# Moving the norm statistic into the projection loop, shifting the dequantising jobs, and a third FC1 weight buffer

## The chip, the cores and the metric

The kernel runs on the 8 cores of one Trainium2 chip, one batch element on each, with no traffic between them. The time is that of the device in microseconds, of the slowest core. Before the change the median of 3 runs is 1756.84 us (1755.2 to 1759.04).

## The reference, cut to what matters

```
x:  8 x 2048 x 1024
xn = layernorm(x)
q, k, v = xn @ Wq, xn @ Wk, xn @ Wv          # 16 heads of 64
q, k = rope(q), rope(k)
s  = softmax(causal(q @ k.T / 8)) @ v @ Wo
h  = layernorm(xn) * gamma + beta
w1 = (fc1_q - 128) * fc1_scales              # 1024 x 4096, int32 and scales per 128 rows
w2 = (fc2_q - 128) * fc2_scales              # 4096 x 1024
g  = silu(xn + 0.5 * (silu(h @ w1 + b1) @ w2 + b2))
out = x + s * g
```

## The kernel before, in words

Everything is issued in an order written out by hand: `sch.op` appends an instruction to one engine's stream, `sch.wait` appends a wait on a semaphore to it, and each engine works its stream in order. A block (`run_block`) ends with all engines meeting.

**Block b2** first projects v, then runs the projection loop (L485 to L558): 8 rounds `it`, 4 for q and 4 for k, each for 4 heads. A round has 4 strips `tgq` of 512 tokens. A strip is 16 matmuls on TensorE (L502, L507), two evacuations on ScalarE (L518, L520), and the rotation on VectorE, six operations (L526 to L541) into `qe_s` and `qo_s`. Strip 2 reuses the PSUM half of strip 0, so its matmuls wait for strip 0's evacuation. After strip 3 ScalarE issues eight DMAs (L550, L553) that put the round's heads in place in `q_att` or `k_att`; VectorE waits for the eight of the round before (L524) before it overwrites `qe_s`. Between rounds SyncE loads the next weights and VectorE casts them (L480).

Then comes the norm loop (L567 to L596), which finds the largest squared norm over pairs of heads for a safe softmax offset. For each of 8 head pairs of q and of k: a Square on ScalarE (L572), four matmuls with ones into `p6` (L579), a `reduce_max` (L585) and a running maximum on VectorE (L593). The Square of one waits for the matmuls of the one before.

**Block b3, attention.** 32 groups (4 query stretches `qg` of 512, 8 head pairs `m`), with K = 4, 8, 12, 16 key tiles a group as `qg` rises. For each key tile TensorE makes the scores (L733), ScalarE the exponentials (L752), GpSimd masks the last 4 tiles of a group (L762, L764), TensorE sums values and denominators (L782, L790). The epilogue of a group is split: its reciprocals (L803) and casts (L808) are queued on VectorE in the next group, and the broadcast matmul (L815), the copy to `rep_sb` (L823) and the product (L827) at that group's end. Between two groups stands a batch of the 48 dequantising jobs: SyncE loads the integers and the scales into one buffer each, VectorE forms the product (L688), GpSimd issues the store (L693). Jobs 0 to 15 are for w1 (2048 columns), 16 to 47 for w2 (1024 columns). A job's VectorE operation waits for the store of the job before, since there is one output buffer. How many jobs are due after group `gidx` is one line:

```
L847  want = min(ndq, (ndq * gidx + 31) // 32)
```

**Block b3, output projection and FC1.** 16 token tiles `tt` of 16 matmuls with Wo (L934, L938); from `tt` 2 on four FC1 visits stand behind each (L914, 8 matmuls of 512 columns), 64 visits in all. A visit needs 256 KB of w1 in one of two buffers `w1t3`, loaded on SyncE's queue once the visit two before is through:

```
L899  if vi >= 2:
L900      sch.wait("sync", "cPE", pe_y[vi - 2])
```

The same stretch loads `h_fm`, `w2a` and `w2b`.

**Block b4** has FC2 for the first 1024 tokens (L1068, L1072), FC1 for the second 1024 (L1038, 32 weight loads into two buffers `w1t`), FC2 for them, and the elementwise end.

Of the kernel before, what the change touches and what calls it, by code (L numbers as in the profile page):

```python
# [7 lines left out]
F32 = mybir.dt.float32  # L8
# [6 lines left out]
S = 2048  # L15
# [3 lines left out]
F = 4096  # L19
# [74 lines left out]
def build_nc(upto=9):  # L94
# [31 lines left out]
    with ExitStack() as es:  # L126
# [239 lines left out]
        with ExitStack() as ps:  # L366
# [83 lines left out]
            rp_t = [sb(ps, f"rp_t{i}", 1024, BF16) for i in range(2)]  # L450
            sch.wait("vector", "cGP", gp_hm[NCH - 1])
# [31 lines left out]

            emit_slab_loads(0)
            for ti, (w_d_, att) in enumerate(((wq_d, q_att), (wk_d, k_att))):  # L485
                for cp in range(4):
                    it = ti * 4 + cp
                    wp = it % 2
                    if it + 1 < 8:
                        emit_slab_loads(it + 1)  # L490
# [3 lines left out]
                    for tgq in range(4):  # L494
# [49 lines left out]
                        gp_rope[(it, tgq)] = sch.snap("cVE")  # L544
                    ve_rope_all = sch.snap("cVE")
# [14 lines left out]
            nsq = [qe_s, qo_s]  # L560
            sch.wait("scalar", "dR0")
            sch.wait("scalar", "dR1")
            sch.wait("scalar", "cVE")
            first_nmax = {0: True, 1: True}
            sc_nsq = {}
            pe_nmm = {}
            for ti, att in enumerate((q_att, k_att)):  # L567
                for m in range(8):
                    im = 8 * ti + m
                    if im >= 1:  # L570
                        sch.wait("scalar", "cPE", pe_nmm[im - 1])
                    sch.op("scalar", lambda e, att=att, m=m, im=im: e.activation(  # L572
                        nsq[im % 2][:], att[:, S * m:S * (m + 1)], AF.Square), inc="cSC")
                    sc_nsq[im] = sch.snap("cSC")
                    sch.wait("tensor", "cSC", sc_nsq[im])
                    if im >= 1:
                        sch.wait("tensor", "cVE")
                    for tgq in range(4):
                        sch.op("tensor", lambda e, tgq=tgq, im=im: e.matmul(  # L579
                            p6[0:1, :], ones_bf[:],  # L580
                            nsq[im % 2][:, 512 * tgq:512 * (tgq + 1)],
                            start=(tgq == 0), stop=(tgq == 3)), inc="cPE")
                    pe_nmm[im] = sch.snap("cPE")
                    sch.wait("vector", "cPE", pe_nmm[im])
                    sch.op("vector", lambda e: e.reduce_max(  # L585
                        stat[:1, 12:13], p6[0:1, :], axis=AX.X), inc="cVE")
                    sch.wait("vector", "cVE")
                    if first_nmax[ti]:
                        sch.op("vector", lambda e, ti=ti: e.tensor_copy(
                            stat[:1, 10 + ti:11 + ti], stat[:1, 12:13]), inc="cVE")  # L590
                        first_nmax[ti] = False
                    else:
                        sch.op("vector", lambda e, ti=ti: e.tensor_max(  # L593
                            stat[:1, 10 + ti:11 + ti],
                            stat[:1, 10 + ti:11 + ti], stat[:1, 12:13]), inc="cVE")
                    sch.wait("vector", "cVE")  # L596
# [27 lines left out]
        with ExitStack() as ps:  # L624
# [7 lines left out]
            lrec = sb(ps, "lrec", 512, F32)  # L632
            lrecb = sb(ps, "lrecb", 512, BF16)
            rep_sb = sb(ps, "rep_sb", 512, F32)
# [14 lines left out]
            with ExitStack() as ds:  # L649
# [58 lines left out]
                for qg in range(NQG):  # L708
                    for m in range(8):
# [137 lines left out]
                        want = min(ndq, (ndq * gidx + 31) // 32)  # L847
# [11 lines left out]
                for eng in ("sync", "vector", "scalar", "gpsimd"):  # L859
                    sch.wait(eng, "cVE", ve_dq_all)  # L860
                    sch.wait(eng, "dG0")
                    sch.wait(eng, "dG1")
            with ExitStack() as ws:
                w1t3 = [sb(ws, f"w1t3_{i}", NCH * 128, BF16) for i in range(2)]
# [31 lines left out]
                def emit_fc1_visit(vi):  # L896
                    ph, oc = fc1_visits[vi]
                    wb = w1t3[vi % 2]
                    if vi >= 2:  # L899
                        sch.wait("sync", "cPE", pe_y[vi - 2])  # L900
                    sch.op("sync", lambda e, oc=oc, wb=wb: e.dma_start(
                        out=wb[:],
                        in_=bass.AP(w1dram, 1024 * oc,
                                    [[NCH * F, 128], [128, 8], [1, 128]])), inc=f"dW{vi % 2}", k=16)
                    dwv = sch.snap(f"dW{vi % 2}")
# [3 lines left out]
                    sch.wait("tensor", f"dW{vi % 2}", dwv)  # L909
# [76 lines left out]
        with ExitStack() as ps:  # L986
# [9 lines left out]
            w1t = [sb(ps, f"w1t{i}", NCH * 128, BF16) for i in range(2)]  # L996
# [7 lines left out]
            for oc in range(2):  # L1004
                sch.op("sync", lambda e, oc=oc: e.dma_start(
                    out=w1t[oc][:],
                    in_=bass.AP(w1dram, 1024 * oc,
                                [[NCH * F, 128], [128, 8], [1, 128]])), inc=f"dW{oc % 2}", k=16)
                dw_pre[oc] = sch.snap(f"dW{oc % 2}")
# [7 lines left out]
            for p in range(NP):  # L1017
                if p == 1:
                    pe_v2 = {}
                    sc_y2 = {}  # L1020
                    for oc in range(NFC):
                        wb = w1t[oc % 2]
                        if oc >= 2:
                            sch.wait("sync", "cPE", pe_v2[(oc - 2, 1)])
# [3 lines left out]
                                            [[NCH * F, 128], [128, 8], [1, 128]])), inc=f"dW{oc % 2}", k=16)  # L1028
                            dw_now = sch.snap(f"dW{oc % 2}")
                        else:  # L1030
                            dw_now = dw_pre[oc]
                        sch.wait("tensor", f"dW{oc % 2}", dw_now)
# [170 lines left out]
```

How the kernel before makes its waits and increments, by code:

```python
            def g(e, fn=fn, h=c.h, k=k):  # L49
                fn(e).then_inc(h, k)
# [4 lines left out]
    def wait(self, eng, name, val=None):  # L55
        c = self.ct[name]
        v = c.n if val is None else val
        self.streams[eng].append(lambda e, h=c.h, v=v: e.wait_ge(h, v))
```

## Time and profile before

| | |
|---|---|
| median of 3 runs | 1756.84 us (1755.2 to 1759.04) |
| the profiled execution | 1761.0 us |
| its span, slowest core (all: 1730.4 to 1759.4) | 1759.4 us |
| TensorE busy with matmuls | 1173.9 us, 67% |
| VectorE busy | 627.5 us, 36% |
| ScalarE busy | 553.9 us, 31% |
| GpSimd busy | 303.9 us, 17% |
| mean granted TensorE clock, by core | 0.834 to 0.840 |

The shares are means over stages with different limits; what a change is worth is read inside the stage that it touches. Positions such as 349.61 are microseconds from the span's start on the slowest core. A number in brackets with an arrow is how long the engine had been idle and whose work it waited for. The granted clock is a mean over a stretch of two levels, 1.2 and 2.4 GHz.

### The profile page before, as it was taken

How to read it: one execution, taken by the hardware profiler on the slowest of the kernel's cores; microseconds unless marked ns; L12 is line 12 of the kernel's file. 1: busy time of each engine (PE TensorE's matmuls, PEld its weight loads, DVE VectorE, ACT ScalarE, POOL GpSimd, SP SyncE). 2: the span in 40 equal slices, each digit the busy share in tenths (PEclk: the TensorE clock that was granted, in tenths of full speed). 3: DMA queues.
4: the chain of work that ended last, by engine and by line, in shares of the span. 5: the costliest groups of instructions: out<-in, count | busy, mean ns of one | idle time of the engine just before them, and what ended most of it. 6: DMA issues, size and time to landing. Idle time of an engine off the chain costs nothing. (4 is left out here: it accounts for less than half of the span.)

```text
span 1759.4 us, 16319 instructions; the slowest of 8 cores (1730.4 to 1759.4 us)
## 1 busy us (share of the span) xinstructions
PE 1173.9 (67%) x5250; PEld 427.6 (24%) x5250; DVE 627.5 (36%) x674; ACT 553.9 (31%) x609; POOL 303.9 (17%) x574
## 2 busy tenths in 40 slices
PE   0004798774423345667877888667887998599994
PEld 0003243331000011111212222223333443244442
DVE  2132645543126666566545444500000112000123
ACT  1133012113422234546767777312122100243000
POOL 0100700000033333232232222300000132100230
PEclk9999999885555556767788888789999999799998
DMA  5655214441075566333322222374533322223223
GB/s 155 124 166 162 89 48 109 103 96 28 0 199 195 183 210 204 118 128 103 108 90 91 90 90 91 118 247 122 165 114 108 126 83 97 86 76 90 69 76 119
DMA packets 83922, 205.72 MB, mean 117 GB/s; under 512 B 16496, under 2 KB 33152, under 8 KB 78464
## 3 DMA queue, kind: packets, MB, share of 16 engines
q1 hardware_dynamic: 66096, 147.51, 27.0%
q10 hardware_dynamic: 8864, 29.38, 5.4%
q0 software_dynamic: 8880, 27.79, 5.1%
q8 instruction: 45, 0.74, 0.2%
q14 instruction: 37, 0.30, 0.1%
HBM read 163.21 MB, written 37.76 MB: 114 GB/s over the span
## 5 line engine op out<-in xcount | busy, mean ns | idle before, releaser
L752 ACT ACTIVATE ptb<-pbig,negub 128x1024 bf16<-128x1024 f32 x320 | 336.3, 1119 | 291.0 <-PE pbig L733 290.8
L782 PE MATMUL p<-ptb,v_tm 128*64 128x512 bf16 x640 | 158.2, 486 | 177.6 <-POOL ptb L764 90.0
L803 DVE RECIPROCAL lrec<-p 1x512 f32<-1x512 f32 x64 | 214.0, 3344 | 1.0
L733 PE MATMUL pbig<-q_att,k_att 64*128 64x512 bf16 x640 | 149.8, 482 | 36.3 <-ACT ptb L752 35.3
L914 PE MATMUL p<-h_fm,w1t 128*128 128x512 bf16 x512 | 129.3, 409 | 52.4 <-DMA w1t<-w1deq 44.3
L790 PE MATMUL p<-ptb,ones_bf 128*1 128x512 bf16 x640 | 146.9, 455 | 0.0
L1093 DVE TENSOR_SCALAR t_f<-xb,negmu_a,r_a 128x1024 f32<-128x1024 f32 x16 | 13.0, 812 | 348.0 <-PE p L1072 205.8
L764 POOL TENSOR_TENSOR ptb<-ptb,msk_bf 128x128 bf16<-128x128 bf16 x256 | 111.0, 439 | 104.8 <-ACT ptb L752 104.6
L1038 PE MATMUL p<-h_fm,w1t 128*128 128x512 bf16 x512 | 113.0, 384 | 22.8 <-ACT y_sl L1046 22.4
L688 DVE SCALAR_TENSOR_TENSOR dq_o<-dq_i,dq_s 128x1024 bf16<-128x1024 int32 (+1 forms) x48 | 75.6, 1575 | 146.7 <-DMA w2deq<-dq_o 68.0
L1119 POOL TENSOR_TENSOR f_sb<-f_sb,sb 128x1024 f32<-128x1024 f32 x13 | 30.5, 2345 | 508.5 <-ACT f_sb L1111 508.5
L332 PE MATMUL pT<-idn_bf,xnb 128*128 128x128 bf16 x128 | 16.2, 306 | 151.8 <-DVE xnb L324 148.7
L782 PEld LDWEIGHTS p<-ptb,v_tm 128*64 128x64 bf16 x640 | 40.7, 114 | 278.8 <-issue 278.8
L923 ACT ACTIVATE y_sl<-p,b_cm 128x512 bf16<-128x512 f32 x64 | 44.0, 687 | 168.6 <-PE p L914 168.5
L502 PE MATMUL pbig<-xn_fm,wE 128*128 128x512 bf16 x256 | 70.6, 425 | 31.9 <-ACT qeo L520 29.1
L1111 ACT ACTIVATE f_sb<-f_sb 128x1024 f32<-128x1024 f32 x16 | 16.9, 1057 | 228.9 <-DVE f_sb L1104 228.9
L914 PEld LDWEIGHTS p<-h_fm,w1t 128*128 128x128 bf16 x512 | 51.4, 104 | 128.3 <-issue 81.1
L1038 PEld LDWEIGHTS p<-h_fm,w1t 128*128 128x128 bf16 x512 | 50.4, 99 | 85.2 <-issue 27.3
L823 DVE COPY rep_sb<-p 128x512 f32<-128x512 f32 x32 | 22.1, 691 | 127.9 <-PE p L815 127.9
L1046 ACT ACTIVATE y_sl<-p,b_cm 128x512 bf16<-128x512 f32 x64 | 43.9, 687 | 73.2 <-PE p L1038 67.5
L507 PE MATMUL pbig<-xn_fm,wO 128*128 128x512 bf16 x256 | 66.5, 407 | 0.0
L733 PEld LDWEIGHTS pbig<-q_att,k_att 64*128 64x128 bf16 x640 | 31.5, 97 | 139.6 <-issue 139.6
(140 smaller groups left out, 1514.1 us busy)
## 6 DMA issues: line engine op xcount, KB each, us to landing
xb<-x SPq DMA_DIRECT2D x48, 512.0 KB, 4.5
w1t<-w1deq SPq DMA_DIRECT2D x96, 256.0 KB, 2.8
dq_i<-fc_q SPq DMA_DIRECT2D x16, 1024.0 KB, 5.5
dq_s<-fc_scales SPq DMA_DIRECT2D x16, 1024.0 KB, 9.0
dq_i<-fc_q SPq DMA_DIRECT2D x32, 512.0 KB, 4.0
dq_s<-fc_scales SPq DMA_DIRECT2D x32, 512.0 KB, 5.0
w1deq<-dq_o POOLq DMA_DIRECT2D x16, 512.0 KB, 9.7
w2deq<-dq_o POOLq DMA_DIRECT2D x32, 256.0 KB, 5.5
```

The source lines that it names most:

```text
L502: sch.op("tensor", lambda e, fc=fc, tgq=tgq, pe_=pe_, wp=wp: e.matmul(pe_, wE[wp][:, 128 * fc:128 * (fc + 1)], xn_fm[:, S * fc + 512 * tgq ...
L507: sch.op("tensor", lambda e, fc=fc, tgq=tgq, po_=po_, wp=wp: e.matmul(po_, wO[wp][:, 128 * fc:128 * (fc + 1)], xn_fm[:, S * fc + 512 * tgq ...
L688: sch.op("vector", lambda e, cols=cols, bi=bi: e.scalar_tensor_tensor(dq_o[bi][:, 0:cols], dq_i[bi][:, 0:cols], -128.0, dq_s[bi][:, 0:cols ...
L733: dst=(sc0 if jj == 0 else sc1): e.matmul(dst, k_att[r:r + 64, S * m + 128 * kt:S * m + 128 * (kt + 1)], q_att[r:r + 64, S * m + 512 * qg: ...
L752: sch.op("scalar", lambda e, pt=pt, half=half: e.activation(pt[:, 0:1024], pbig[:, 1024 * half:1024 * half + 1024], AF.Exp, bias=negub[:, ...
L764: sch.op("gpsimd", lambda e, pt=pt, base=base, off=off: e.tensor_mul(pt[:, base + off:base + off + 128], pt[:, base + off:base + off + 128 ...
L782: K=K, gp=gp: e.matmul(obank[gp][cpos:cpos + 64, :], v_tm[:, 1024 * kt + 64 * h:1024 * kt + 64 * (h + 1)], pt[:, 512 * (cpos // 64):512 * ...
L790: sch.op("tensor", lambda e, pt=pt, jj=jj, kt=kt, K=K, gp=gp: e.matmul(bass.AP(lbank[gp], 32 * jj * 512, [[512, 1], [1, 512]]), ones_bf[:] ...
L803: sch.op("vector", lambda e, jj=jj, gp=gp: e.reciprocal(lrec[32 * jj:32 * jj + 1, :], bass.AP(lbank[gp], 32 * jj * 512, [[512, 1], [1, 512 ...
L914: sch.op("tensor", lambda e, fc=fc, ph=ph, wb=wb, yp=yp: e.matmul(yp[:], wb[:, 128 * fc:128 * (fc + 1)], h_fm[:, S * fc + 512 * ph:S * fc ...
L923: sch.op("scalar", lambda e, oc=oc, ph=ph, yp=yp: e.activation(y_sl[:, 1024 * oc + 512 * ph:1024 * oc + 512 * (ph + 1)], yp[:], AF.Silu, b ...
L1038: sch.op("tensor", lambda e, fc=fc, ph=ph, wb=wb, yp=yp: e.matmul(yp[:], wb[:, 128 * fc:128 * (fc + 1)], h_fm[:, S * fc + 1024 + 512 * ph: ...
```

## The change

Four edits. **A.** The sixteen norms leave the loop of their own: in round `it` of the projection loop, from 1 on, the two norms of round `it - 1` are made, the first Square at the head of the round in ScalarE's stream, the rest after strip 1 is queued; the last two stay behind the loop. There is one scratch buffer `nsq_b`. **B.** The number of jobs due after a group follows another rule. **C.** The FC1 weights of block b3 rotate over three buffers, in space given back by `lrec`, `lrecb` and `rep_sb`. **D.** The same in block b4.

```diff
+            nsq_b = sb(ps, "nsq_b", S, BF16)
...
+            def emit_norm_sq(itx):
+                ti_x, cp_x = itx // 4, itx % 4
+                att_x = q_att if ti_x == 0 else k_att
+                for j2 in range(2):
+                    im = 8 * ti_x + 2 * cp_x + j2
+                    m = 2 * cp_x + j2
+                    if im >= 1:
+                        sch.wait("scalar", "cPE", pe_nmm[im - 1])
+                    sch.wait("scalar", f"dR{itx % 2}", dr_rep[(itx, 3)])
+                    sch.op("scalar", lambda e, att_x=att_x, m=m: e.activation(
+                        nsq_b[:], att_x[:, S * m:S * (m + 1)], AF.Square), inc="cSC")
+                    sc_nsq[im] = sch.snap("cSC")
+                    break
+
+            def emit_norm_mm(itx, j2):
...
+                if j2 == 1:
+                    if im >= 1:
+                        sch.wait("scalar", "cPE", pe_nmm[im - 1])
+                    sch.op("scalar", lambda e, att_x=att_x, m=m: e.activation(
+                        nsq_b[:], att_x[:, S * m:S * (m + 1)], AF.Square), inc="cSC")
+                    sc_nsq[im] = sch.snap("cSC")
+                sch.wait("tensor", "cSC", sc_nsq[im])
+                if im >= 1:
+                    sch.wait("tensor", "cVE", ve_nrm[im - 1])
+                for tgq in range(4):
+                    sch.op("tensor", lambda e, tgq=tgq: e.matmul(
+                        p6[0:1, :], ones_bf[:],
+                        nsq_b[:, 512 * tgq:512 * (tgq + 1)],
+                        start=(tgq == 0), stop=(tgq == 3)), inc="cPE")
+                pe_nmm[im] = sch.snap("cPE")
+                sch.wait("vector", "cPE", pe_nmm[im])
+                sch.op("vector", lambda e: e.reduce_max(
+                    stat[:1, 12:13], p6[0:1, :], axis=AX.X), inc="cVE")
+                sch.wait("vector", "cVE")
...
+                ve_nrm[im] = sch.snap("cVE")
...
                     wp = it % 2
+                    if it >= 1:
+                        emit_norm_sq(it - 1)
...
                         gp_rope[(it, tgq)] = sch.snap("cVE")
+                        if tgq == 1 and it >= 1:
+                            emit_norm_mm(it - 1, 0)
+                            emit_norm_mm(it - 1, 1)
...
-            for ti, att in enumerate((q_att, k_att)):
-                for m in range(8):
...
+            emit_norm_sq(7)
+            emit_norm_mm(7, 0)
+            emit_norm_mm(7, 1)
...
-                        want = min(ndq, (ndq * gidx + 31) // 32)
+                        if gidx <= 12:
+                            want = min(ndq, gidx // 3)
+                        else:
+                            want = min(ndq, 4 + (gidx - 12) * (ndq - 4) // 20)
...
+            ax.close()
             with ExitStack() as ws:
-                w1t3 = [sb(ws, f"w1t3_{i}", NCH * 128, BF16) for i in range(2)]
+                w1t3 = [sb(ws, f"w1t3_{i}", NCH * 128, BF16) for i in range(3)]
...
-                    if vi >= 2:
-                        sch.wait("sync", "cPE", pe_y[vi - 2])
+                    if vi >= 3:
+                        sch.wait("sync", "cPE", pe_y[vi - 3])
+                    else:
+                        sch.wait("sync", "cVE", ve_oevac_prev)
...
-            w1t = [sb(ps, f"w1t{i}", NCH * 128, BF16) for i in range(2)]
+            w1t = [sb(ps, f"w1t{i}", NCH * 128, BF16) for i in range(3)]
...
-                        if oc >= 2:
-                            sch.wait("sync", "cPE", pe_v2[(oc - 2, 1)])
+                        if oc >= 3:
+                            sch.wait("sync", "cPE", pe_v2[(oc - 3, 1)])
```

## Rows read from the trace of the kernel before

**Rows 1.** Stretches: length, busy PE, PEld, DVE, ACT, POOL (instructions), granted clock, DMA share, GB/s.

```profile
250.00:411.20 161.20, 127.72 (x512) 53.23 (x512) 83.87 (x206) 35.27 (x65) 0.00 (x0) 0.87 0.37 92
411.20:487.90 76.70, 29.98 (x66) 6.00 (x68) 13.81 (x36) 31.24 (x19) 0.00 (x0) 0.50 0.06 14
1133.50:1371.90 238.40, 184.24 (x768) 76.78 (x769) 20.61 (x32) 45.26 (x65) 9.54 (x18) 0.93 0.51 157
```

**Rows 2.** Timeline, TensorE, projection loop: start, duration, what, idle before.

```profile
275.93 3.57 PE L502 MATMUL pbig<-xn_fm,wE 128*128 128x512 bf16 x8 [5.02 <-ACT qeo L520]
...
281.31 1.89 PE L502 MATMUL pbig<-xn_fm,wE 128*128 128x512 bf16 x8
...
295.46 1.89 PE L502 MATMUL pbig<-xn_fm,wE 128*128 128x512 bf16 x8 [3.62 <-ACT qeo L520]
...
356.02 3.57 PE L502 MATMUL pbig<-xn_fm,wE 128*128 128x512 bf16 x8 [3.61 <-ACT qeo L520]
...
362.31 1.89 PE L502 MATMUL pbig<-xn_fm,wE 128*128 128x512 bf16 x8
```

**Rows 3.** Timeline, ScalarE, projection loop: first DMA of rounds 0, 4, 5, 7.

```profile
269.45 0.60 ACTq L550 DMA_DIRECT2D q_att<-qe_s  x1
...
349.61 0.53 ACTq L550 DMA_DIRECT2D k_att<-qe_s  x1
...
370.03 0.53 ACTq L550 DMA_DIRECT2D k_att<-qe_s  x1
...
411.22 0.51 ACTq L550 DMA_DIRECT2D k_att<-qe_s  x1
```

**Rows 4.** A rotation's group on VectorE; norm loop: first Square and reduce, last Square.

```profile
L526 DVE TENSOR_TENSOR rp_t<-qeo,cos_sb 128x512 bf16<-128x512 bf16 x32 | 13.5, 421 | 19.0 <-ACT qeo L520 9.0 <-DMA k_att<-qo_s 7.0 <-DMA q_att<-qo_s 3.0
...
418.13 1.91 ACT L572 ACTIVATE qe_s<-q_att 128x2048 bf16<-128x2048 bf16 x1 [9.77 <-DMA k_att<-qo_s]
...
422.16 0.68 DVE L585 TENSOR_REDUCE stat<-p 1x1 f32<-1x512 f32 x1 [11.02 <-PE p L579]
...
479.87 1.91 ACT L572 ACTIVATE qo_s<-k_att 128x2048 bf16<-128x2048 bf16 x1 [2.21 <-PE p L579]
```

**Rows 5.** Timeline, VectorE, attention, and the groups of the dequantising jobs.

```profile
530.40 0.69 DVE L823 COPY rep_sb<-p 128x512 f32<-128x512 f32 x1 [1.72 <-PE p L815]
...
543.84 0.69 DVE L823 COPY rep_sb<-p 128x512 f32<-128x512 f32 x1 [1.73 <-PE p L815]
...
569.24 0.69 DVE L823 COPY rep_sb<-p 128x512 f32<-128x512 f32 x1 [1.05 <-PE p L815]
...
725.77 0.69 DVE L823 COPY rep_sb<-p 128x512 f32<-128x512 f32 x1 [1.15 <-PE p L815]
...
740.19 0.69 DVE L823 COPY rep_sb<-p 128x512 f32<-128x512 f32 x1 [4.09 <-PE p L815]
...
759.48 0.69 DVE L823 COPY rep_sb<-p 128x512 f32<-128x512 f32 x1 [1.12 <-PE p L815]
...
964.43 0.69 DVE L823 COPY rep_sb<-p 128x512 f32<-128x512 f32 x1 [12.77 <-PE p L815]
...
1120.84 0.69 DVE L823 COPY rep_sb<-p 128x512 f32<-128x512 f32 x1 [4.17 <-PE p L815]
...
1131.94 0.69 DVE L823 COPY rep_sb<-p 128x512 f32<-128x512 f32 x1 [0.89 <-PE p L815]
...
L688 DVE SCALAR_TENSOR_TENSOR dq_o<-dq_i,dq_s 128x1024 bf16<-128x1024 int32 x32 | 39.0, 1219 | 75.4 <-DMA w2deq<-dq_o 68.0 <-DMA w1deq<-dq_o 7.4
L688 DVE SCALAR_TENSOR_TENSOR dq_o<-dq_i,dq_s 128x2048 bf16<-128x2048 int32 x16 | 36.6, 2287 | 71.3 <-DMA w1deq<-dq_o 57.7 <-DMA dq_s<-fc_scales 13.6
```

**Rows 6.** Groups of FC1 matmuls, and one burst in the timeline of TensorE.

```profile
L914 PE MATMUL p<-h_fm,w1t 128*128 128x512 bf16 x512 | 129.3, 409 | 52.4 <-DMA w1t<-w1deq 44.3 <-DMA h_fm<-h_spill 8.0
...
1259.39 5.30 PE L914 MATMUL p<-h_fm,w1t 128*128 128x512 bf16 x16 [2.15 <-DMA w1t<-w1deq]
...
L1038 PE MATMUL p<-h_fm,w1t 128*128 128x512 bf16 x512 | 113.0, 384 | 22.8 <-ACT y_sl L1046 22.4 <-DMA w1t<-w1deq 0.4
```

More of the change, by code:

```diff
@@ L482, in emit_slab_loads @@
                     ve_slab[(it, pi)] = sch.snap("cVE")
+            first_nmax = {0: True, 1: True}
+            sc_nsq = {}
+            pe_nmm = {}
+            ve_nrm = {}
+            def emit_norm_sq(itx):
[11 more added lines that the diff above has]
+                    break
@@ new lines, in emit_norm_mm @@
+            def emit_norm_mm(itx, j2):
+                ti_x, cp_x = itx // 4, itx % 4
+                att_x = q_att if ti_x == 0 else k_att
+                im = 8 * ti_x + 2 * cp_x + j2
+                m = 2 * cp_x + j2
+                if j2 == 1:
[17 more added lines that the diff above has]
+                sch.wait("vector", "cVE")
+                if first_nmax[ti_x]:
+                    sch.op("vector", lambda e, ti_x=ti_x: e.tensor_copy(
+                        stat[:1, 10 + ti_x:11 + ti_x], stat[:1, 12:13]), inc="cVE")
+                    first_nmax[ti_x] = False
+                else:
+                    sch.op("vector", lambda e, ti_x=ti_x: e.tensor_max(
+                        stat[:1, 10 + ti_x:11 + ti_x],
+                        stat[:1, 10 + ti_x:11 + ti_x], stat[:1, 12:13]), inc="cVE")
+                ve_nrm[im] = sch.snap("cVE")
@@ L558, in build_nc @@
                     pe_qk[it] = sch.snap("cPE")
[L560 to L566, printed above, removed]
-            for ti, att in enumerate((q_att, k_att)):
-                for m in range(8):
[L569 to L596, printed above, removed]
+            emit_norm_sq(7)
+            emit_norm_mm(7, 0)
+            emit_norm_mm(7, 1)
             sch.wait("scalar", "cVE")
@@ L631, in build_nc @@
             pt_b = [sb(ps, f"ptb{i}", 2048, BF16) for i in range(3)]
-            lrec = sb(ps, "lrec", 512, F32)
-            lrecb = sb(ps, "lrecb", 512, BF16)
-            rep_sb = sb(ps, "rep_sb", 512, F32)
+            ax = ExitStack()
+            lrec = sb(ax, "lrec", 512, F32)
+            lrecb = sb(ax, "lrecb", 512, BF16)
+            rep_sb = sb(ax, "rep_sb", 512, F32)
             sch = Sched(cts)
@@ L908, in emit_fc1_visit @@
                         sch.wait("tensor", "dG0", dh_sw)
-                    sch.wait("tensor", f"dW{vi % 2}", dwv)
+                    sch.wait("tensor", f"dW{vi % 3}", dwv)
                     yp = p6 if vi % 2 == 0 else p7
@@ L1003, in build_nc @@
             dw_pre = {}
-            for oc in range(2):
+            for oc in range(3):
                 sch.op("sync", lambda e, oc=oc: e.dma_start(
@@ L1007, in build_nc @@
                     in_=bass.AP(w1dram, 1024 * oc,
[L1008 to L1009 removed]
+                                [[NCH * F, 128], [128, 8], [1, 128]])), inc=f"dW{oc % 3}", k=16)
+                dw_pre[oc] = sch.snap(f"dW{oc % 3}")
             pe_z = {}
@@ L1027, in build_nc @@
                                 in_=bass.AP(w1dram, 1024 * oc,
-                                            [[NCH * F, 128], [128, 8], [1, 128]])), inc=f"dW{oc % 2}", k=16)
-                            dw_now = sch.snap(f"dW{oc % 2}")
+                                            [[NCH * F, 128], [128, 8], [1, 128]])), inc=f"dW{oc % 3}", k=16)
+                            dw_now = sch.snap(f"dW{oc % 3}")
                         else:
                             dw_now = dw_pre[oc]
-                        sch.wait("tensor", f"dW{oc % 2}", dw_now)
+                        sch.wait("tensor", f"dW{oc % 3}", dw_now)
                         for ph in range(2):
```

9 lines of the change are left out of this document (5 added, 4 removed).

## The prediction, made before the changed kernel was run

> **What bounds the kernel now.** I read the busy time of each engine over stretches first, to cut the span into stages, then the timeline inside each stage that the change touches, and the groups of instructions for what ends the waits. No one engine bounds the kernel: each stage has its own limit [rows 1]. The stretch 250.0 to 411.2 is the projection loop (TensorE 127.7 of 161.2 us busy, granted clock 0.87), 411.2 to 487.9 the norm loop (clock 0.50, no engine near full), 487.9 to 1133.5 the attention, which VectorE's and TensorE's meeting points pace [rows 5], 1133.5 to 1371.9 the output projection with the first half of FC1 (clock 0.93). The groups of instructions then say what ends the idle time in that last stage and in the block after it.
>
> **Edit A, the norms into the projection loop.** *Removed:* in the norm loop one Square starts every 4.12 us: sixteen from 418.13 to 479.87 [rows 4]. Fourteen of the sixteen rounds go, the last two stay: 14 x 4.12 = 57.7 us off the path.
>
> *Added:* seven of the eight loop rounds get two norms of the round before. Let t = 0 be the first of ScalarE's eight transposing DMAs. Now: first DMA at 349.61, next round's at 370.03, so 20.3 us a round (seven rounds from 269.45 to 411.22) [rows 3]. Inside it ScalarE issues its eight DMAs and evacuates strip 0, which TensorE waits for until 356.02 = +6.4, when it starts strip 2, strip 3 at 362.31 = +12.7, and 7.7 us later the next round's DMAs are issued [rows 2, 3]. After:
> 1. ScalarE's first Square waits for the DMAs to land. In the last round they are issued from 411.22 on and the Square that waits for them starts at 418.13, +6.9; it takes 1.9: until +8.9 [rows 3, 4]. Behind it in ScalarE's queue stand the evacuations, so strips 0 and 1 are done at about +10.1 and +11.1 (0.5 us for each of two halves; strip 0 is now done at +6.3). SP's and POOL's queues are passed by nothing here.
> 2. TensorE does the first norm's four matmuls at +9.0. The second norm needs p6 back, and the reduce that frees it stands in VectorE's queue behind the rotations of strips 0 and 1 (2.6 us each: 10.1 to 15.3). The rotations of a strip are six operations of 0.42 us each; reduce (0.68) and maximum end at +16.3 [rows 4].
> 3. The second norm's matmuls start at +16.4; only behind them stand strips 2 and 3 in TensorE's queue. Four cold matmuls take 1.7 us, so strip 2 starts at +18.1 instead of +6.4. This is a new wait that replaces the old one: what was late was ScalarE's evacuation, what is late next is VectorE's reduce, and TensorE's matmuls queue behind it.
> 4. Clock. Eight matmuls take 3.57 us as a row at the 1.2 GHz level and 1.89 at 2.4 GHz, which is 0.43 and 0.22 us from one to the next. TensorE now idles 3.61 us before strip 2, whose sixteen matmuls then take 362.31 - 356.02 = 6.3 us: 13 of them, 5.7 us, cold. After a gap of 5.02 us they took 281.31 - 275.93 = 5.4: cold for 3.9 us [rows 2]. After, it idles twice a round (6 us before the first norm, 5.4 before the second), so it is cold from +16.4 for 3.9 to 5.8 us. Strip 2 ends, and strip 3 starts, at +22.7 to +23.6. With the same 7.7 us behind it the round takes 30.4 to 31.3 us.
> So 7 x (30.9 - 20.3) = +74.2, less 57.7: **A costs 16.5 us**. All warm throughout, the round is 16.4 + 0.9 + 3.5 + 7.7 = 28.5 us and A costs nothing (-1 at best); both strips wholly cold, 16.4 + 1.7 + 6.8 + 6.8 + 4.2 = 35.9, and A costs 51.
>
> **Edit B, dequantisation later.** From one evacuation of `rep_sb` to the next, VectorE does a batch of jobs and the reciprocals; TensorE does one group; both meet at the epilogue. So an interval is the longer of the two. VectorE without jobs: 543.84 - 530.40 = 13.4 with one w1 job of 2.28, so 11.2 [rows 5]. A second w1 job waits for the first one's store: 569.24 - 543.84 = 25.4 (mean of four such intervals 26.2), so 12.8 for each w1 job after the first. Two w2 jobs: 759.48 - 740.19 = 19.3, and 8.0 for a third (10 waits of 68.0 us in all, plus the job's 1.22) [rows 5]. TensorE's own pace: K=8 14.4 (740.19 - 725.77, 4.1 us of it VectorE waiting); K=16 (1120.84 - 964.43) / 7 = 22.3, where VectorE waits 12.8 us after one job and 4.2 after two [rows 5]. K=4 is taken as under 11.2: its group fitted into 13.4 although its masks stood behind the job's store on POOL's queue.
>
> The pacing now gives 2, 1, 2, 1 ... jobs. After it gives one after groups 3, 6, 9, 12, then two each, three after 17, 22, 27 and 32. Counted from 487.9: two groups 22.4; four empty intervals 44.8; two with a w1 job 26.9; five at K=8 pace 72.0; four of two w1 jobs 104.8; three w1 39.0; one mixed 22 (11.2 + 2.3 + a 7.4 us wait + 1.2); four of two w2 77.2; one of three w2 27.3; seven at K=16 pace 156.4; one of three there 27.3; and the last 27, because its three jobs stand before the last reciprocals with no matmuls left to hide them (before: one job, about 11). Sum 647, against 1131.94 - 487.9 = 644.0 now: **B costs 3 us**. It gains some 85 us by group 12 and gives them all back: stalls of a second job rise from 16 to 24, nine of them under K=16 groups. Bounds: -10 (K=8 groups at VectorE's 11.2 to 13.4) to +15 (each K=16 interval and each w1 job after a first 0.8 us longer; the four intervals behind 26.2 spread from 25.4 to 27.2).
>
> **Edit C, a third FC1 weight buffer in the output-projection stage.** 44.3 us of TensorE's idle time there ends with a w1 load, 21 times [rows 6]. In a steady burst of four visits the third waits 2.15 until 1259.39 [rows 6]. Its load was asked for when the first visit ended, one visit (1.73, eight matmuls) before that wait began, so request to use is 3.9 us; I take 4.0. With three buffers the third visit's load is there, and the fourth's comes at 1.73 + 4.0 = 5.7 where 5.2 is wanted: 0.5 us of stall instead of 2.2. Thirteen bursts keep 6.5, the first (5.6 us, beside the w2a and h_fm loads) keeps 4, and the tail of plain visits keeps none (1.73 + 4.0 over three buffers is 1.9 a visit, near the 1.73 of its matmuls). 44.3 - 10.5 = 33.8; I take **-32**, since more outstanding loads lengthen each. Bounds: -20 (request to use 5 us) to -38 (some cold matmuls gone too). The new wait of SP's queue for `ve_oevac_prev` is over when the output projection starts, which needs the same value: nothing. The smaller scratch stack moves no work.
>
> **Edit D, the third buffer in the last block.** Loads end 0.4 us of waiting in the FC1 half there; 22.4 ends with ScalarE [rows 6]. One more 256 KB load stands on SP before the first x load, under 13 us of FC2 matmuls: 0.4 at most either way, taken as 0.
>
> **Sum:** +16.5 + 3 - 32 = -12.5 us. The profiled execution took 1761.0 us (span 1759.4), 4.2 above the median of the runs: 1761.0 - 12.5 = 1748.5, and in terms of the median 1756.84 - 12.5 = **1744.3 us**.
>
> **Rivals.**
> - *The clock holds in the projection loop.* For it: after 3.62 us idle before 295.46 the matmuls stayed at full rate [rows 2]. Against: the six others went cold, the one at 356.02 after the same gap. A is 0, the time 1728.
> - *Slower: both strips stay cold.* Idle, 1.7 us of work, idle again, and TensorE does not get its clock back before strip 3 ends; the round is 35.9 us, A costs 51, the time is 1779. It decides the sign from 1.8 us a round beyond my 30.9. For it: in the norm loop, at 1.9 us of matmuls in 4.12, the clock stayed at 0.50 throughout [rows 1, 4]. Against: after each single gap it came back within 6 us. The Trainium skill (TensorE: Matmul & The Clock Gate, "HAM oscillation") says that gaps between bursts leave every burst cold; the trace agrees for the first 5.8 us and not for the rest.
> - *Late batches cost more.* The third job holds POOL's queue, so the masks of a K=16 group start late and its tail is bare; w1 stores slow one another in the four pairs. B is +15, the time 1756. For it: the spread of 1.8 us among equal intervals above. Against: after two jobs a K=16 group has 4.2 us to spare [rows 5].
> - *The loads are bound by transfer, not by buffers.* Then request to use grows with the third buffer and C gives 10: 1766. For it: DMA share 0.51 over that stage [rows 1]. Against: 4.0 us is steady from burst to burst.
> - *The early gain is kept.* K=8 groups at VectorE's pace: B -10, the time 1731.
>
> **Numbers.** Forecast 0.52 (its own range 1735 to 1753), clock holds 0.12, both strips cold 0.11, late batches 0.12, transfer-bound 0.07, early gain 0.06. About 0.2% (3.5 us) is what a measurement of this kernel can tell from no change. Faster: 0.48 of the forecast, both gains and a little of the late batches, 0.69. Same: the rest of the forecast and most of the late batches, 0.11. Slower: 0.20. The range leaves out the cold strips and part of the clock case: 1724 to 1767.
>
> **What would show it.** A: rounds of 30 to 31 us between the first transposing DMAs, strip 2 some 18 us into the round behind a wait on VectorE's maximum, two Squares left after the loop. B: reciprocals of group 12 near 85 us earlier counted from the attention's start, the lead gone at its end, a bare stretch of VectorE before the last epilogue. C: waits on w1 loads near 10 us. The prediction is wrong if the rounds stay near 28 or reach 35, if the K=8 groups with two w1 jobs are not at 26, or if waits on w1 loads stay above 25.

## The result, and the profile after

Ten executions of the changed kernel have a median of 1735.66 us, ten of the kernel before 1757.39 us on the same chip; the ratio is 0.9883, with a 95% interval of 0.9859 to 0.9907. So the change is 20.5 us faster (16 to 25). The forecast was 12.5 us faster, at 1744.3 us. Ratios here and below leave disturbed executions out, which is why a ratio can differ from that of two medians.

The four edits lie in different stages, so the first thing to read is how long each stage is, as a mean over the eight cores. The limits are the first matmul of the projection loop, of the scores, of the output projection (Wo), of FC2, and the last of FC2:

```
stage, us                          before   after   difference   edit, forecast
projection loop and norms           236.8   261.6     +24.8       A  +16.5
attention                           641.5   636.8      -4.7       B   +3
output projection, first FC1        235.4   195.2     -40.2       C  -32
last block, to the last FC2         365.7   364.1      -1.6       D    0
```

The sum is -21.7, near the 20.5 of the ratio. The stages come from the one profiled execution of each kernel. A and C have the sign that was forecast and B has not; of the sizes only D's, near nothing, is as forecast.

The stretches of the kernel after, on its slowest core (columns as in [rows 1]):

```profile
247.00:411.20 164.20, 95.67 (x381) 38.05 (x388) 66.59 (x162) 43.13 (x55) 0.00 (x0) 0.79 0.30 71
411.20:510.40 99.20, 52.89 (x185) 19.45 (x190) 32.15 (x83) 22.55 (x29) 0.00 (x0) 0.72 0.19 43
510.40:1146.80 636.40, 423.46 (x1984) 103.18 (x1985) 365.08 (x240) 337.77 (x321) 196.69 (x504) 0.71 0.43 136
1146.80:1342.00 195.20, 172.63 (x752) 75.08 (x768) 20.60 (x32) 44.86 (x65) 9.54 (x18) 0.96 0.61 191
```

The last row answers to the third of [rows 1]: 195.2 us for 238.4, granted clock 0.96 for 0.93, 191 GB/s for 157. The first two answer to its first two: the stretch of clock 0.50 is gone, and the loop that took its work runs at a granted clock of 0.79 and 0.72.

**Edit A in the trace.** One round of the projection loop, from its first transposing DMA to that of the next, in the timeline of all engines:

```profile
328.87 0.54 ACTq L609 DMA_DIRECT2D q_att<-qe_s  x1
...
336.97 1.91 ACT L499 ACTIVATE nsq_b<-q_att 128x2048 bf16<-128x2048 bf16 x1 [10.95 <-DMA q_att<-qo_s]
...
339.13 1.87 PE L519 MATMUL p<-nsq_b,ones_bf 128*1 128x512 bf16 x4 [7.45 <-ACT nsq_b L499]
...
341.09 1.91 ACT L512 ACTIVATE nsq_b<-q_att 128x2048 bf16<-128x2048 bf16 x1 [0.27 <-PE p L519]
...
344.79 0.43 DVE L597 TENSOR_TENSOR qo_s<-rp_t 128x512 bf16<-128x512 bf16 x1
345.14 0.67 DVE L525 TENSOR_REDUCE stat<-p 1x1 f32<-1x512 f32 x1
345.91 0.15 DVE L533 TENSOR_TENSOR stat<-stat 1x1 f32<-1x1 f32 x1
...
346.21 1.86 PE L519 MATMUL p<-nsq_b,ones_bf 128*1 128x512 bf16 x4 [5.21 <-DVE stat L533]
...
348.40 2.00 PE L558 MATMUL pbig<-xn_fm,wE 128*128 128x512 bf16 x7 [0.33 <-issue]
...
351.96 1.89 PE L558 MATMUL pbig<-xn_fm,wE 128*128 128x512 bf16 x8
...
359.68 0.53 ACTq L609 DMA_DIRECT2D q_att<-qe_s  x1
```

The chain is the one of the forecast's steps 1 to 3, link by link: landing, Square, the first norm's matmuls, the rotations of strips 0 and 1 on VectorE, reduce, maximum, the second norm's matmuls, and only behind them strip 2. The second Square was done at 343.0, and TensorE still waited for VectorE until 346.2. Of strip 2's first eight matmuls seven are recorded; by the weight loads the first one starts at 348.0. The times from t = 328.87: Square +8.1 (forecast +6.9), maximum's end +17.2 (+16.3), second norm +17.3 (+16.4), strip 2 +19.1 (+18.1), next round +30.8 (+30.9). The seven rounds on this core take 30.3, 30.9, 30.8, 33.4, 33.8, 33.7 and 30.9 us, mean 31.97; by core the mean is 31.2 to 32.5.

**Edit B in the trace.** VectorE's timeline around group 12 and at attention's end:

```profile
654.73 0.69 DVE L849 COPY rep_sb<-p 128x512 f32<-128x512 f32 x1 [3.02 <-PE p L841]
...
669.48 0.69 DVE L849 COPY rep_sb<-p 128x512 f32<-128x512 f32 x1 [3.09 <-PE p L841]
...
685.52 2.29 DVE L714 SCALAR_TENSOR_TENSOR dq_o<-dq_i,dq_s 128x2048 bf16<-128x2048 int32 x1 [12.32 <-DMA w1deq<-dq_o]
...
696.64 0.69 DVE L849 COPY rep_sb<-p 128x512 f32<-128x512 f32 x1 [1.05 <-PE p L841]
```

```profile
1119.28 0.69 DVE L849 COPY rep_sb<-p 128x512 f32<-128x512 f32 x1 [4.40 <-PE p L841]
...
1120.68 1.22 DVE L714 SCALAR_TENSOR_TENSOR dq_o<-dq_i,dq_s 128x1024 bf16<-128x1024 int32 x1
1128.02 1.23 DVE L714 SCALAR_TENSOR_TENSOR dq_o<-dq_i,dq_s 128x1024 bf16<-128x1024 int32 x1 [6.13 <-DMA w2deq<-dq_o]
1135.47 1.22 DVE L714 SCALAR_TENSOR_TENSOR dq_o<-dq_i,dq_s 128x1024 bf16<-128x1024 int32 x1 [6.22 <-DMA w2deq<-dq_o]
1136.61 6.72 DVE L829 RECIPROCAL lrec<-p 1x512 f32<-1x512 f32 x2
...
1145.18 0.69 DVE L849 COPY rep_sb<-p 128x512 f32<-128x512 f32 x1 [0.89 <-PE p L841]
```

The epilogue of group 12 is at 669.48, which is 159.1 us after attention's start at 510.4, where before it was at 252.3 on the profiled core: a lead of 93 us. The next interval, with two w1 jobs, is 27.2 long, 12.3 of it a wait for a store. The second fence is the bare stretch before the last epilogue: 25.9 us with three jobs in it. By then the lead is all but spent: the last epilogue comes 634.8 us after attention's start, against 644.0 in [rows 5].

**Edit C in the trace.** The group of the first FC1's matmuls (497 of the 512 are recorded), then a burst of visits in TensorE's timeline:

```profile
L946 PE MATMUL p<-h_fm,w1t 128*128 128x512 bf16 x497 | 117.4, 386 | 21.7 <-DMA w1t<-w1deq 12.6 <-DMA h_fm<-h_spill 8.1 <-issue 0.2
```

```profile
1252.35 5.34 PE L946 MATMUL p<-h_fm,w1t 128*128 128x512 bf16 x23
1258.17 1.89 PE L946 MATMUL p<-h_fm,w1t 128*128 128x512 bf16 x8 [0.47 <-DMA w1t<-w1deq]
```

Waits on w1 loads are 12.6 us for 44.3 [rows 6], and in a burst three visits run through and the fourth waits 0.47, where the forecast said 0.5. What it did not say is in the other column: a matmul takes 386 ns on average instead of 409, and 24 matmuls (23 recorded) now fit in 5.34 us where 16 took 5.30.

### The profile page after: what moved, and what is told of

Same layout as the page of the kernel before. It is cut to its first block and busy times, and to the rows that moved or that the text cites. A ratio compares the mean times of both kernels' runs of the same rounds, so it can differ in the third digit from the quotient of the medians.

```text
span 1728.6 us, 16245 instructions; the slowest of 8 cores (1716.4 to 1728.6 us)
## 1 busy us (share of the span) xinstructions
PE 1159.4 (67%) x5186; PEld 425.7 (25%) x5250; DVE 629.7 (36%) x674; ACT 553.3 (32%) x609; POOL 305.1 (18%) x574
## 5 line engine op out<-in xcount | busy, mean ns | idle before, releaser
L829 DVE RECIPROCAL lrec<-p 1x512 f32<-1x512 f32 x64 | 214.0, 3344 | 13.3 <-PE p L816 12.3
L946 PE MATMUL p<-h_fm,w1t 128*128 128x512 bf16 x497 | 117.4, 386 | 21.7 <-DMA w1t<-w1deq 12.6
L1070 PE MATMUL p<-h_fm,w1t 128*128 128x512 bf16 x502 | 112.6, 385 | 21.6 <-ACT y_sl L1078 20.9
L519 PE MATMUL p<-nsq_b,ones_bf 128*1 128x512 bf16 x64 | 29.8, 620 | 108.9 <-ACT nsq_b L499 69.8
L759 PEld LDWEIGHTS pbig<-q_att,k_att 64*128 64x128 bf16 x640 | 31.8, 98 | 139.5 <-issue 139.5
L788 POOL MEMSET ptb<- 128x128 bf16 (+2 forms) x192 | 59.8, 312 | 20.7 <-ACT ptb L778 20.5
## 6 DMA issues: line engine op xcount, KB each, us to landing
dq_s<-fc_scales SPq DMA_DIRECT2D x16, 1024.0 KB, 10.1
```

The source lines that it names most:

```text
L759: dst=(sc0 if jj == 0 else sc1): e.matmul(dst, k_att[r:r + 64, S * m + 128 * kt:S * m + 128 * (kt + 1)], q_att[r:r + 64, S * m + 512 * qg: ...
L829: sch.op("vector", lambda e, jj=jj, gp=gp: e.reciprocal(lrec[32 * jj:32 * jj + 1, :], bass.AP(lbank[gp], 32 * jj * 512, [[512, 1], [1, 512 ...
```

## The experiments

Each kernel was timed against the kernel before on the same chip. Stage lengths are means over the eight cores of one profiled execution:

```
us                        ratio   interval         loop+norms  attention  Wo+FC1  last
before                                              236.8       641.5     235.4   365.7
A alone                  1.0151  1.0128 - 1.0174    261.0       639.7     236.5   365.8
B alone                  0.9962  0.9946 - 0.9978    236.8       635.6     236.8   366.9
C alone                  0.9762  0.9748 - 0.9776    237.6       640.5     194.4   365.7
D alone                  1.0002  0.9989 - 1.0014    236.7       641.2     237.5   365.2
A, weights left out      one run                    252.6       640.7     236.9   364.6
A, second bank           1.0032  1.0014 - 1.0050    240.5       641.4     237.4   366.3
A, norms late            0.9640  0.9615 - 0.9666    173.9       643.1     235.9   365.9
flat pacing              0.9594  0.9569 - 0.9618    236.7       569.8     238.4   373.0
C, four buffers          0.9724  0.9621 - 0.9827    237.1       642.6     181.9   366.1
late, flat, 3 buffers    0.8978  0.8954 - 0.9003    172.8       568.5     195.8   365.7
late, flat, 4 buffers    0.8892  0.8854 - 0.8930    174.7       567.8     182.4   365.7
```

**One edit at a time.** The first four kernels are the kernel before with one edit of the change each.

A alone:

> The kernel before with edit A alone (norms into the projection loop, the one scratch row nsq_b; no new pacing, no third buffer). The forecast's own term: +16.5 us against before, rounds 30.9 us. The theory read from the combined kernel: its rounds 3 to 5 were 33 to 34 us because the rotation's DMAs land 8 to 10 us after their issue where the next round's weights load beside them, not 6.9; that gives +25 us, projection stage 262 us on every core. Rival: A is dearer only together with the other edits (other memory addresses, another start of attention); then A alone is near +16 and the stage near 253.

It is 26.5 us slower (ratio 1.0151; 22.5 to 30.6), the stage 24.2 us longer, rounds 31.5 to 32.1 us in the mean by core, where before they are 19.9 to 20.3. A costs the same without the other edits; the rival falls.

B alone:

> The kernel before with edit B alone (the want formula of the dequantizing jobs). Forecast's term: +3 us (between -10 and +15). Reading of the combined kernel: attention 4.7 us shorter, because an interval without a job is 10.0 us long and not 11.2 and one with two w2 jobs 18.4 to 19.2; so -5 us. Rival: the shortening of attention in the combined kernel comes from edit A (it starts attention with VectorE free and a warm clock); then B alone is at 0 to +3. Either way the lead at the epilogue of group 12 should be 85 to 95 us against before, and gone at the last group.

It is 6.7 us faster (3.9 to 9.5), attention 5.9 us shorter. B's gain is its own, not A's.

C and D alone:

> The kernel before with the first half of edit C/D alone: a third weight buffer in the first FC1 phase (b3). Forecast's term: -32 us, out of waits alone. Reading of the combined kernel: stage b3 40 us shorter, 32 of it waits and 8 of it matmuls that no longer run cold after a wait; so -40 us, mean FC1 matmul near 386 ns against 409. Rival: the 8 us come from what the other edits left behind (w1 already dequantized sooner, another phase of the cores); then C alone is at -32.

> The kernel before with the third weight buffer in the last block (b4) alone. Forecast's term: 0, since FC1b's waits there are short. Reading of the combined kernel: the stage is 1.6 us shorter. So between -2 and 0. Rival: with the loads further ahead they collide with the output's or h's transfers and it costs a few us.

C is 41.8 us faster (39.4 to 44.3), the stage 41.0 us shorter; D is 1.0002, nothing. What the waits and the clock gave is read from the matmuls' group and the stretch of the stage, on the slowest core of C alone:

```profile
L918 PE MATMUL p<-h_fm,w1t 128*128 128x512 bf16 x497 | 117.6, 386 | 23.5 <-DMA w1t<-w1deq 12.9 <-DMA h_fm<-h_spill 8.3 <-ACT y_sl L927 1.3
```

```profile
1128.70:1326.80 198.10, 172.57 (x752) 75.06 (x769) 20.62 (x32) 45.28 (x65) 9.57 (x18) 0.96 0.61 189
```

Waits for w1 fall by 44.3 - 12.9 = 31.4, and the clock rises to 0.96 with nothing else changed. So the stage gets some 10 us from the clock on top of the waits. The four ratios multiply to 0.987, the changed kernel's is 0.988: no interaction of the edits shows beyond the intervals.

**Why A costs 24 and not 16: the landing.** In A alone the weights of rounds 2 to 7 are not loaded (those rounds use the weights of rounds 0 and 1, so the values differ; the matmuls, rotations and norms are all there):

```diff
-                    for fc in range(NCH):
+                    for fc in range(NCH if it < 2 else 0):
```

> Edit A alone, with the projection's weight loads of rounds 2 to 7 left out (these rounds use the weights of rounds 0 and 1, so the values differ; all other work is the same). Theory: the rotation's DMAs land 8 to 10 us after their issue because the weight loads of the next round share the queues; without them they land near 6.9 us, rounds of 30 to 31 us throughout, projection stage 250 to 255 us against 262. Rival: the landing depends on the place of the DMA's writes and on the other cores, not on the weight loads; then the landing stays at 8 to 10 us and the stage near 262.

The line of the first Square of a round, in A alone and then in A without the loads, on core 2 of each:

```profile
L499 ACT ACTIVATE nsq_b<-q_att x4: 1909/1910/1910, 274.6 to 369.4; 128x2048 bf16<-128x2048 bf16 x4
L499 ACT ACTIVATE nsq_b<-k_att x4: 1909/1910/1910, 402.3 to 493.5; 128x2048 bf16<-128x2048 bf16 x4
its engine sat idle before it (us, times) until:
  DMA q_att<-qo_s: 46.7, 4
  DMA k_att<-qo_s: 41.7, 4
```

```profile
  DMA q_att<-qo_s: 38.9, 4
  DMA k_att<-qo_s: 38.8, 4
```

ScalarE's idle time before these eight Squares falls by 10.7 us. The Square comes at +6.8 to +6.9 in every round, where with the loads it comes at +8.0 to +9.7 in the first six and at +6.9 in the seventh, beside which no loads run. Over all eight cores it is +6.7 to +6.9 without loads, and +7.4 to +9.7 beside them. The stage is 8.4 us shorter and its excess over before is 15.8 us, near the forecast's 16.5. So the mis-sized term is the landing of step 1: I had read it from the last round, beside which no loads run. The kernel before was not run without its loads, so what they cost its own rounds is not known, and 15.8 is A's cost only if they cost those nothing.

TensorE's timeline of one round of that kernel, core 2, from the first norm on:

```profile
335.56 1.87 PE L519 MATMUL p<-nsq_b,ones_bf 128*1 128x512 bf16 x4 [6.21 <-ACT nsq_b L499]
342.64 1.86 PE L519 MATMUL p<-nsq_b,ones_bf 128*1 128x512 bf16 x4 [5.22 <-DVE stat L533]
344.44 3.59 PE L558 MATMUL pbig<-xn_fm,wE 128*128 128x512 bf16 x8
347.82 1.96 PE L563 MATMUL pbig<-xn_fm,wO 128*128 128x512 bf16 x8
349.62 1.89 PE L558 MATMUL pbig<-xn_fm,wE 128*128 128x512 bf16 x8
```

Here all eight first matmuls of strip 2 are at the 1.2 GHz level, as step 4 said; in the round shown above, after a gap of 7.45 us and one of 5.21, they were so only in part. From the second norm's start to strip 3's it is 349.62 - 342.64 = 6.98 us here and 351.96 - 346.21 = 5.75 there, and both rounds take 30.8: 1.3 us of later landing against 1.2 us less of cold matmuls. In this pair the one hid the other. Over the 56 rounds of each kernel (seven on each of eight cores) the stretch from the second norm to strip 3 is 5.7 to 7.4 us, mean 6.5, in A alone, and 6.1 to 7.2, mean 6.8, without the loads: 0.2 us a round on average.

**The wait on VectorE's maximum.** The same place in A alone, but the second norm has a PSUM bank of its own:

```diff
-                if im >= 1:
-                    sch.wait("tensor", "cVE", ve_nrm[im - 1])
+                if im >= 2:
+                    sch.wait("tensor", "cVE", ve_nrm[im - 2])
...
-                        p6[0:1, :], ones_bf[:],
+                        nbank[j2][0:1, :], ones_bf[:],
```

> Edit A alone with a second PSUM bank for the second norm of a round, at the same place in the program: its matmuls wait for the second Square and not for VectorE's maximum of the first. With A alone rounds were 31.8 us. If VectorE's maximum sets the second norm (the forecast's step 4), its matmuls come at about +14 us and not +17 in each of seven rounds, and the kernel is 15 to 25 us faster than with A alone, 1762 to 1770 us, projection stage near 240. Rival: the second Square, which waits for the first norm's matmuls to free the one scratch row, and the evacuation of strip 1 by ScalarE behind it, set strip 2 anyway; then under 1 us a round, 1780 us or more.

Core 2, TensorE:

```profile
331.27 1.86 PE L520 MATMUL p<-nsq_b,ones_bf 128*1 128x512 bf16 x4 [7.44 <-ACT nsq_b L500]
335.48 1.86 PE L520 MATMUL p<-nsq_b,ones_bf 128*1 128x512 bf16 x4 [2.35 <-DVE rp_t L586]
337.28 2.89 PE L560 MATMUL pbig<-xn_fm,wE 128*128 128x512 bf16 x8
```

The second norm starts 4.2 us after the first, not 7.1 (the row names a rotation on VectorE; the event that came last is the second Square's end). The stage is 240.5 us against 261.0, and the kernel at 1.0032 against 1.0151: 21 us of A's cost were this one wait, 20.5 / 7 = 2.9 us a round. The forecast's steps 2 and 3 named it, and it is most of A's cost, though not its sign: with it gone, A still costs 3.7 us of stage instead of 24, and the ratio stays above 1.

**The norms where nobody waits.** Two scratch rows and two banks; ScalarE squares behind its evacuations of strips 1 and 2, TensorE's norm matmuls stand behind strip 3, the maxima behind the rotation of strip 3:

```diff
-                    if it >= 1:
-                        emit_norm_sq(it - 1)
...
+                        if tgq in (1, 2) and it >= 1:
+                            emit_norm_sq(it - 1, tgq - 1)
...
-                        if tgq == 1 and it >= 1:
-                            emit_norm_mm(it - 1, 0)
-                            emit_norm_mm(it - 1, 1)
...
+                    if it >= 1:
+                        for j2 in range(2):
+                            emit_norm_mm(it - 1, j2)
+                        for j2 in range(2):
+                            emit_norm_max(it - 1, j2)
```

> Edit A placed otherwise: two scratch rows and two PSUM banks, the Squares of the round before behind ScalarE's evacuations of strips 1 and 2, all norm matmuls behind strip 3, the maxima behind the rotation of strip 3. No engine should wait for a norm. Theory (A costs time through its place alone, since strip 2 stands behind the chain landing, Square, matmuls, maximum): rounds of 21 to 23 us, 50 to 57 us of norms gone after the loop, -35 to -50 us against before, 1707 to 1722 us. Rival: eight more small matmuls and two Squares a round cost their time wherever they stand (4 to 6 us a round, since the loop is bound by ScalarE's and VectorE's sum); then -10 to -25 us.

Core 2, TensorE:

```profile
323.81 1.89 PE L551 MATMUL pbig<-xn_fm,wE 128*128 128x512 bf16 x8 [1.69 <-ACT qeo L569]
...
330.81 1.02 PE L509 MATMUL p<-nsq,ones_bf 128*1 128x512 bf16 x4
332.65 1.02 PE L509 MATMUL p<-nsq,ones_bf 128*1 128x512 bf16 x4 [0.81 <-DVE qo_s L592]
333.61 1.90 PE L551 MATMUL pbig<-xn_fm,wE 128*128 128x512 bf16 x8
```

It is 63 us faster than before (59 to 68), more than the -50 that I expected at best. The rounds are 19.3 to 19.9 us in the mean by core, against 19.9 to 20.3 with no norms in them: the gap before strip 2 is now 1.69 us instead of 3.6, and the strip is warm. The stretch of the seven rounds on core 2, before and then here (columns as in [rows 1]):

```profile
265.00:406.00 141.00, 111.28 (x427) 45.81 (x433) 73.49 (x181) 29.65 (x56) 0.00 (x0) 0.85 0.39 96
262.00:397.00 135.00, 109.39 (x472) 44.86 (x472) 82.86 (x206) 54.90 (x70) 0.00 (x0) 0.96 0.39 96
```

Work that nobody waits for costs nothing here, and with it in the gaps the granted clock is 0.96 instead of 0.85; at the 2.4 GHz level four norm matmuls take 1.02 us instead of 1.86.

**The pacing of the jobs.** In the kernel before:

```diff
-                        want = min(ndq, (ndq * gidx + 31) // 32)
+                        want = min(ndq, gidx if gidx <= 15 else 15 + 2 * (gidx - 15))
```

> The kernel before with another pacing of the dequantizing jobs: one after each group up to 15, then two after each. Theory: the first job of a group is free (an interval without a job is 10.0 to 11.2 us and with one w1 job 13 to 14.4 at K=4, the rest lies under the matmuls at K=8 and K=16), each further job at one place stalls TensorE by its own 8 to 13 us, so what matters is how many stand second at K=4 and K=8, and not how early the jobs are done. With no second job before K=12 attention comes out 40 to 75 us shorter, 1685 to 1715 us. Rival: a job costs the same wherever it stands, because VectorE is the bound over the whole stage; then attention's length stays within 10 us.

Attention is 71.7 us shorter and the kernel 71 us faster (67 to 76). The line of the dequantising products, in B alone and then with the flat pacing, each on its slowest core:

```profile
L689 DVE SCALAR_TENSOR_TENSOR dq_o<-dq_i,dq_s 128x1024 bf16<-128x1024 int32 (+1 forms) x48 | 75.7, 1577 | 192.1 <-DMA w2deq<-dq_o 108.6 <-DMA w1deq<-dq_o 76.1 <-DMA dq_s<-fc_scales 7.4
```

```profile
L688 DVE SCALAR_TENSOR_TENSOR dq_o<-dq_i,dq_s 128x1024 bf16<-128x1024 int32 (+1 forms) x48 | 75.7, 1576 | 126.3 <-DMA w2deq<-dq_o 89.4 <-DMA dq_s<-fc_scales 19.7 <-DMA w1deq<-dq_o 17.2
```

Waits for w1 stores are 17 us instead of 76: no w1 job stands second in a batch. At group 12 this kernel is at 179 us from attention's start, behind B alone at 157 and ahead of before at 251; at the end it is at 568, where B alone is at 634 and before at 640. So the early lead is no measure. Nor is the bare count of jobs that stand second in a batch: it is 16 in this pacing and 16 in the kernel before. What differs is where they stand. In the kernel before, in the mean over eight cores, an interval with two w1 jobs is 26.5 us against 13.7 with one at K=4, and 26.0 against 14.3 at K=8; with two w2 jobs it is 18.6 against 18.1 at K=12, and 22.6 against 22.1 at K=16. The flat pacing has all its second jobs but one in the cheap places. Its last block is 373.0 us long because of two cores with a lower granted clock, of which more in the last section.

**A fourth weight buffer**, in C alone (`range(4)`, `vi % 4`, `vi - 4`):

> Edit C alone with four weight buffers in the first FC1 phase where it has three; three gave 1715 us, with 11 to 13 us of waits for weights left in the stage. If the number of buffers still bounds the loads, most of these waits go: 1703 to 1708 us, stage 185 us. If the transfers bound them (DMA share .61 in the stage at three buffers, the waits at the start of the stage and every third visit alike), a fourth only moves the waits: 1712 to 1718 us.

```profile
L918 PE MATMUL p<-h_fm,w1t 128*128 128x512 bf16 x512 | 114.9, 383 | 13.2 <-DMA h_fm<-h_spill 9.5 <-DMA w1t<-w1deq 3.8
```

The stage is 181.9 us against 194.4, 178 to 186 by core against 189 to 198; waits for w1 are 3.8 us on the slowest core. The ratio's interval (0.9621 to 0.9827) holds that of three buffers, so the stage decides: the loads were bound by buffers still. The pair below confirms it.

**All together.**

> The norms placed late (two scratch rows, two banks), the flat pacing of the jobs, and three weight buffers in both phases, together. The parts alone gave -63, -70, -42 and 0 us. If they add up: 1757 - 175 = 1582 us. Rivals: denser matmuls lower the granted clock (in the flat pacing's run two cores ran the last block at .81 to .84 and took 396 us for it where the others took 365), which puts 20 to 40 us on: 1600 to 1625 us; or the flat pacing, which leaves the last w2 jobs close to the end of attention, collides with the earlier weight loads; 1590 to 1600 us.

> The same with four weight buffers in both phases. Buffer-bound: 8 to 12 us under the version with three; transfer-bound: within 3 us of it.

Ratios 0.8978 and 0.8892: 180 and 195 us faster than before, 15 us apart by the fourth buffer. The parts alone summed to 63 + 71 + 42 = 176 for the first; they add up, and neither rival came true, the last block being 365.7 us as before. The version with four buffers is the fastest of all, with a median of 1567.26 us against 1763.41 beside it, and its granted clock is 0.870 to 0.884 by core.

## Why the prediction held, and where its steps were off

The mechanisms held, and none of the signs that were to show the prediction wrong came: the rounds are 30.1 to 34.1 us, the four intervals with two w1 jobs in a row 26.4 in the mean, the waits on w1 loads 12.6. The sizes were off: the net of -12.5 against -20.5 is three errors that partly cancel. By each edit's own run A was forecast 10 us too cheap, B 10 too dear and C 10 too small. That the total came within 8 us of the forecast is partly luck, since A's error took back one of the other two.

- **A, removed.** Two Squares were left behind the loop, as forecast. Nothing was off here: in A alone the rounds are 31.8 us for 20.1 in the mean over cores, 7 x 11.7 = 81.9, and 81.9 - 57.7 is the 24.2 that the stage grew.
- **A, steps 2 and 3.** The new wait on VectorE's maximum was there in each of the seven rounds, and removing it alone gave back 20.5 us of stage. Shown.
- **A, step 1, landing +6.9.** This is the term that was mis-sized. With the next round's weights loading it is 7.4 to 10.1; without them it is 6.7 to 6.9 and the stage's excess is 15.8. Shown.
- **A, step 4, clock.** From the second norm's start to strip 3's it was 5.7 to 7.4 us in the changed kernel, mean 6.5, where the forecast had 6.3 to 7.2 and a warm engine 4.4. So the term was right to a few tenths, a little too dear. The rival that the clock holds is out, and so is the one of two cold strips: strip 3 was warm. The Trainium skill (TensorE: Matmul & The Clock Gate, "HAM oscillation") says that the work behind each such gap starts cold, every time; the trace agrees with it for the head of each burst, 1.86 us for the four norm matmuls, and strip 3 was back at the 2.4 GHz level, 1.89 us for eight.
- **B.** The mechanism held (lead of 94.5 us at group 12 in the mean over cores of B alone, forecast 85; gone at the end), but the sum came out at 634 where it was forecast at 647. Three terms carry it: four empty K=4 intervals took 39.7 us and not 44.8 (9.9 each; I had 11.2, by subtracting the job's 2.28 us from an interval with one, but with a job such an interval is 13.3 and so 3.4 longer), five K=8 intervals 68.6 and not 72.0, eight around K=12 188.2 and not 191.7. The K=16 intervals (157.6 for 156.4) and the last one (26.3 for 27) were right. And the yardstick, 644.0, was one core's; the mean of eight before is 639.9, which by itself would have made the forecast +7. So the two errors have opposite signs, 13 and 4 us. The rival of late batches is out: a K=16 interval with three jobs is 26.5 us, 27.3 having been forecast. So the sign of B was missed by the size of these terms, and not by an effect that was left out.
- **C.** The wait fell to 12.6, forecast 10.5, and a burst's stall to 0.47, forecast 0.5. Mis-sized is what the waits drag along: TensorE cooled down in them. The forecast left that to its bound of -38, and -41.8 is beyond the bound. It also took 2 us off because more outstanding loads would lengthen each; they do a little: over the stage's 64 loads the median from issue to landing is 2.9 us with two buffers, 3.1 with three and 3.4 with four, in the mean over cores. The rival of transfer-bound loads is out by the fourth buffer: the stage then moves 204 to 211 GB/s by core, where with three it moved 188 to 199.
- **D.** Nothing, as forecast.

Where the cycles of the 1.2 GHz level were lost is shown by granted clock and mean duration beside an otherwise equal kernel. That the rotation's DMAs are slowed by sharing queues with the loads, and not by the loads' traffic at the memory, is not shown; leaving the loads out takes away both.

## What to carry to other kernels

Price a moved step by the last link of its chain on the engine that everyone waits for, and read each link's duration in a stretch where the same neighbours are at work: a landing time from a round without loads was 0.5 to 3 us short. Before moving work into a loop, ask for whom each of its results is awaited; the same norms cost 24 us of stage in one place and gained 63 in another. When jobs stall on one output buffer, price each second job by how much it lengthens the interval that it stands in (here 12 to 13 us for a w1 job at K=4 or K=8, about 0.5 for a w2 job at K=12 or K=16) instead of by how early all are done, and put the second ones where that is least. When waits on loads vanish, count on the clock's share too.

## What the runs showed of the hardware

- The rotation's eight DMAs land 6.7 to 6.9 us after the first is issued when nothing loads beside them, and 7.4 to 10.1 us after when the next round's weights load beside them (A alone, the changed kernel and the one without loads, all cores). The slowest seen was beside all four edits, 10.1; in A alone 9.7.
- In the flat pacing's run cores 0 and 1 ran the first FC2 at a granted clock of 0.81 but for its first 3 us, with 134.2 us for its 512 matmuls, while core 2, on the same die, took 114.7 at 0.99. Their last block took 396 us, that of the other six 364 to 368. TensorE's timeline, core 0 and then core 2, one matmul a row:

```profile
1342.03 0.43 PE L1072 MATMUL p<-w2b,y_sl 128*128 128x512 bf16 x1
1342.29 0.44 PE L1068 MATMUL p<-w2b,y_sl 128*128 128x512 bf16 x1
```

```profile
1340.39 0.38 PE L1072 MATMUL pbig<-w2b,y_sl 128*128 128x512 bf16 x1
1340.61 0.38 PE L1068 MATMUL pbig<-w2b,y_sl 128*128 128x512 bf16 x1
```

  From one matmul to the next it is 0.26 us on the one and 0.22 on the other. So 0.81 is a level of its own there, between the two, and not a mean of them. Cores 2 and 3 had it in the same execution too, but at other times: core 2 from 208 to 293 us of its span, where core 0 is at 0.95. In the other twelve profiles no core is under 0.97 in the first FC2, though all eight run dense matmuls. The Trainium skill (TensorE: Matmul & The Clock Gate, Part 1) tells of a limit at 13/16 of full clock that takes a whole die once three of its cores run dense matmuls; the figure agrees with this trace, the extent (in FC2 two cores of four) and the frequency (one profile of thirteen) don't. Its cause stays open.
- A longer gap did not mean more cold matmuls: after gaps of 6.21 and 5.22 us it took 6.98 us from the second norm to strip 3, after 7.45 and 5.21 us 5.75. In A alone the first gap is 7.3 to 9.8 us in the rounds beside loads, and the same stretch takes anything from 5.7 to 7.4. What sets it stays open.
